# Rotary tables scaled once per layer, the norms' rounding and remainder on other engines, and ScalarE's squares ahead of its mask

## The reference

```python
# stacked: x = x + 0.5 * ffn_stack(layernorm(x)); x = x + ssm_block(layernorm(x)); x = x + 0.5 * ffn_stack(layernorm(x))
# x is (8, 256, 128); DIM = 128, DEPTH = 6, HEADS = 16, DIM_HEAD = 64, WINDOW = 32, QK_SCALE = 8.0
def attn_layer(x, Wqkv, qs, ksc, Wo):
    q, k, v = jnp.split(x @ Wqkv, 3, -1)          # heads of 64
    q = l2norm(q) * qs                            # norm over each head's 64 values, then a scale per layer and feature
    k = l2norm(k) * ksc
    q = q * cos * scale + rotate_half(q) * sin * scale
    k = k * cos * inv + rotate_half(k) * sin * inv          # inv = 1 / scale
    out = local_attention(q, k, v)                # windows of 32 queries, the window's and the previous window's keys
    return out @ Wo

def local_attention(q, k, v):
    sim = jnp.einsum('bhwie,bhwje->bhwij', bq, bk2) * QK_SCALE
    sim = jnp.where(mask, -jnp.finfo(sim.dtype).max, sim)
    attn = jax.nn.softmax(sim, -1)
    return jnp.einsum('bhwij,bhwje->bhwie', attn, bv2)

for i in range(DEPTH):
    x = attn_layer(shift_tokens(x), Wqkv[i], q_scale[i], k_scale[i], Wo[i]) + x
    x = ffn_layer(shift_tokens(x), ln_g[i], ln_b[i], W1[i], b1[i], W2[i], b2[i]) + x
```

## Time and profile before

| what | value |
|---|---|
| median of three runs | 3386.6 us |
| lowest, highest run | 3373.16, 3394.69 us |
| span of the profiled execution | 3373.6 us |
| TensorE (PE) busy | 2905.4 us, 86% |
| VectorE (DVE) busy | 2981.4 us, 88% |
| ScalarE (ACT) busy | 2061.4 us, 61% |
| GpSimd (POOL) busy | 2425.2 us, 72% |
| mean granted TensorE clock | 0.938 |

### The profile page before, as it was taken

How to read it: one execution, slowest core, us unless ns; L and a number is a source line. 1 busy time by engine, 2 the same in 40 slices (tenths; PEclk the granted TensorE clock), 3 DMA queues, 4 the chain that set the end, 5 groups by cost and what they waited for, 6 DMA issues and landing times. The chain is left out here.

```text
span 3373.6 us, 132100 instructions
## 1 busy us (share of the span) xinstructions
PE 2905.4 (86%) x57914; PEld 1846.3 (55%) x57914; DVE 2981.4 (88%) x4200; ACT 2061.4 (61%) x3820; POOL 2425.2 (72%) x1679
## 2 busy tenths in 40 slices
PE   5788889989989899987767788998999988999987
PEld 3455555655655555653323455565566655565653
DVE  6789899999999899896898878989999989899994
ACT  3466566666666665664764456666666666566663
POOL 3678777787787687774454667778788787787773
PEclk8899999999999999998887889999999999999998
DMA  5233332333333333320001333333343333333330
GB/s 140 65 83 73 82 91 68 89 90 72 86 92 71 84 85 71 83 72 28 7 7 44 80 72 79 75 87 86 75 97 76 90 84 72 81 94 71 86 76 14
DMA packets 114726, 250.85 MB, mean 74 GB/s; under 512 B 27244, under 2 KB 60648, under 8 KB 114152
## 3 DMA queue, kind: packets, MB, share of 16 engines
q1 hardware_dynamic: 114152, 242.40, 30.3%
HBM read 37.82 MB, written 3.15 MB: 12 GB/s over the span
## 5 line engine op out<-in xcount | busy, mean ns | idle before, releaser
L1085 ACT ACTIVATE squares<-general 128x512 f32<-128x512 f32 x768 | 453.9, 597 | 720.8 <-PE general L658 712.2
L1279 POOL TENSOR_TENSOR probs<-probs,row_sum 128x1024 f32<-128x1024 f32 x192 | 365.3, 1903 | 426.3 <-DVE row_sum L957 425.5
L1259 POOL TENSOR_TENSOR q_ring<-q_ring,partner 128x512 f32<-128x512 f32 x384 | 491.1, 1279 | 216.6 <-DMA partner<-sines 216.3
L868 DVE SCALAR_TENSOR_TENSOR sines<-general,vec,consts 128x512 f32<-128x512 f32 x768 | 560.7, 730 | 68.4 <-ACT squares L1085 65.5
L1259 POOL TENSOR_TENSOR k_ring<-k_ring,partner 128x512 f32<-128x512 f32 x384 | 490.8, 1278 | 0.0
L692 PE MATMUL general<-probs_t,v_buf 32*64 32x64 f32 x24576 | 339.4, 236 | 158.3 <-issue 87.0
L656 PE MATMUL general<-xs_hi,wqkv_lo 128*128 128x512 f32 x768 | 457.3, 595 | 15.8 <-DVE xs_lo L897 7.6
L692 PEld LDWEIGHTS general<-probs_t,v_buf 32*64 32x64 f32 x24576 | 305.6, 135 | 248.8 <-issue 241.7
L1273 POOL TENSOR_TENSOR probs<-probs,q_scale 128x1024 f32<-128x1024 f32 x192 | 365.3, 1903 | 15.1
L668 PE MATMUL general<-att,wo 128*128 128x512 f32 x768 | 370.4, 627 | 6.5 <-ACT att L1155 5.2
L719 PE MATMUL general<-k_ring,q_ring 64*32 64x64 f32 (+1 forms) x24576 | 294.2, 224 | 88.4 <-issue 53.5
(11 more groups left out here) (232 smaller groups left out, 6348.2 us busy)
## 6 DMA issues: line engine op xcount, KB each, us to landing
partner<-sines SPq DMA_DIRECT2D x1536, 128.0 KB, 2.3
wqkv_raw<-in_wqkv SPq DMA_DIRECT2D x80, 208.0 KB, 2.7
wo<-in_wo SPq DMA_DIRECT2D x12, 512.0 KB, 5.1
w<-in_w SPq DMA_DIRECT2D x12, 341.0 KB, 3.2
base_dram<-x SPq DMA_DIRECT2D x8, 256.0 KB, 2.4
att<-in_wqkv SPq DMA_DIRECT2D x2, 1024.0 KB, 6.1
sines<-base_dram SPq DMA_DIRECT2D x8, 256.0 KB, 4.0
w<-in_w SPq DMA_DIRECT2D x12, 128.0 KB
```

The costliest lines, as they stand in the source:

```text
L868: e.scalar_tensor_tensor(out=by_seq(sines[:, i % 2, which, :]), in0=g, scalar=scale, in1=both(tables[:, 2 * which + 1, :]), op0=ALU.mult, ...
L1085: e.activation(squares[:, (2 * p + which) % 4, :], general_of(("proj", k, n, p, which))[:, :], ACT.Square).then_inc(S[f"squared_{side}"], 1)
L1259: e.tensor_tensor(y, y, partner[:, i % 2, which, :], ALU.add).then_inc(S[f"rotated_{side}"], 1)
L1279: e.tensor_tensor(y, y, spread_keys(row_sum[:, i % 2, :]), ALU.mult).then_inc(S["probs_done"], 1)
```

## The change

It has three parts.

First, the product of rotary table and per-layer scale is made once per layer: `dve_tables` writes `layer_tables` (two tables of 256 columns each for queries, and two for keys, at the first item of a layer), and the four rotary instructions of a step become plain tensor_tensor products with it. `inv_norm` becomes a part of `k_inv`, and the state-space weights `mw` and `wbc` are loaded into `wqkv_raw`, after the last projection weights of the first stack have been split; their DMAs move on SP's queue from before the first stack's steps to behind them.

Second, ScalarE writes the rounded root itself (`high`, an activation with `F32R` output) and the root beside it, both ahead of the eight roots for the queries; GpSimd subtracts (`pool_norms_low`, behind `pool_scores`); VectorE only transposes, and that later in its step, behind `dve_turn`. `dve_var` and `dve_norms`, which overwrite `norm_t`, now also wait until the queries' scales of the item before have been read from it (`q_scaled`).

Third, in each step ScalarE squares the queries' projection first and writes the mask afterwards.

```diff
-xs_hi xs_lo proj_q proj_k squared_q squared_k cos_q cos_k sin_q sin_k moved0 moved1 rotated_q rotated_k
+xs_hi xs_lo tables_scaled proj_q proj_k squared_q squared_k cos_q cos_k sin_q sin_k moved0 moved1 rotated_q rotated_k
...
+        layer_tables = sb("layer_tables", [P, 4, SEQ])
...
-        inv_norm = sb("inv_norm", [P, COLS])
+        inv_norm = k_inv[:, WIN:]
...
-        mw = sb("mw", [P, 4, P])
-        wbc = sb("wbc", [P, P])
+        raw_words = wqkv_raw.rearrange("p i c -> p (i c)")
+        mw = raw_words[:, 0:4 * P].rearrange("p (m n) -> p m n", m=4)
+        wbc = raw_words[:, 4 * P:5 * P]
...
+            if k == 0:
+                w.wait_ge(S["wqkv_lo"], DEPTH * PAIRS)
+                e.dma_start(mw, mw_in.rearrange("m d n -> d m n")).then_inc(S["m_loaded"], 16)
+                e.dma_start(wbc, wb_in).then_inc(S["m_loaded"], 16)
+                e.dma_start(mvec[:, :], mvec_in).then_inc(S["m_loaded"], 16)
...
+        def dve_tables(e, w, k, layer, which):
+
+            w.wait_ge(S["vec_loaded"], 16)
+            w.wait_ge(S[f"cos_{SIDE[which]}"], (k * ITEMS + layer * CHUNKS) * PAIRS)
+            cut = slice(2 * which, 2 * which + 2)
+            e.tensor_scalar(layer_tables[:, cut, :], tables[:, cut, :], vcol(layer, V_QS + which), None, ALU.mult)\
+                .then_inc(S["tables_scaled"], 1)
+
         def dve_rotate(e, w, k, n, p, which):
...
-            g, scale = by_seq(general_of(("proj", k, n, p, which))[:, :]), vcol(layer, V_QS + which)
-            w.wait_ge(S["vec_loaded"], 16)
+            g = by_seq(general_of(("proj", k, n, p, which))[:, :])
+            if p == 0 and n % CHUNKS == 0:
+                dve_tables(e, w, k, layer, which)
+            w.wait_ge(S["tables_scaled"], 2 * (k * DEPTH + layer) + which + 1)
             w.wait_ge(S[f"squared_{side}"], i + 1)
...
-            e.scalar_tensor_tensor(out=by_seq(sines[:, i % 2, which, :]), in0=g, scalar=scale, in1=both(tables[:, 2 * which + 1, :]),
-                                   op0=ALU.mult, op1=ALU.mult).then_inc(S[f"sin_{side}"], 1)
+            e.tensor_tensor(by_seq(sines[:, i % 2, which, :]), g, both(layer_tables[:, 2 * which + 1, :]), ALU.mult).then_inc(S[f"sin_{side}"], 1)
...
-            e.scalar_tensor_tensor(out=by_seq(qk_ring[which][:, slot_of(n, p), :]), in0=g, scalar=scale,
-                                   in1=both(tables[:, 2 * which, :]), op0=ALU.mult, op1=ALU.mult).then_inc(S[f"cos_{side}"], 1)
+            e.tensor_tensor(by_seq(qk_ring[which][:, slot_of(n, p), :]), g, both(layer_tables[:, 2 * which, :]), ALU.mult).then_inc(S[f"cos_{side}"], 1)
...
+            w.wait_ge(S["q_scaled"], m * 8)
...
         def dve_norms_back(e, w, k, n):
 
             m = k * ITEMS + n
-            w.wait_ge(S["k_root"], m + 1)
-            root, low, high = (norm_t[:, :, i * NORM_ROWS:(i + 1) * NORM_ROWS] for i in range(3))
-            e.tensor_copy(high.bitcast(F32R), root).then_inc(S["norms_high"], 1)
-            w.wait_ge(S["norms_high"], m + 1)
-            e.tensor_tensor(low, root, high, ALU.subtract).then_inc(S["norms_low"], 1)
             w.wait_ge(S["norms_low"], m + 1)
-            w.wait_ge(S["inv_parts"], m)
-            e.transpose(inv_norm[:, :], norm_t.rearrange("p w h -> p (w h)")).then_inc(S["k_norms_turned"], 1)
+            w.wait_ge(S["k_norms_off"], 2 * m * GROUPS)
+            e.transpose(inv_norm, norm_t.rearrange("p w h -> p (w h)")).then_inc(S["k_norms_turned"], 1)
...
         def act_norms(e, w, k, n):
             m = k * ITEMS + n
             w.wait_ge(S["sums_inverted"], m + 1)
+            inverse, low, high, root = (norm_t[:, :, i * NORM_ROWS:(i + 1) * NORM_ROWS] for i in range(4))
+            e.activation(high.bitcast(F32R), inverse, ACT.Sqrt).then_inc(S["norms_high"], 1)
+            e.activation(root, inverse, ACT.Sqrt).then_inc(S["k_root"], 1)
...
-            w.wait_ge(S["q_scaled"], (m + 1) * 8)
-            e.activation(norm_t[:, :, 0:NORM_ROWS], norm_t[:, :, 0:NORM_ROWS], ACT.Sqrt).then_inc(S["k_root"], 1)
...
             for st in PLAN:
+                if st.now:
+                    act_square(e, w, k, *st.now, 0)
                 if st.scores:
                     act_mask(e, w, k, *st.scores)
-                if st.now:
-                    act_square(e, w, k, *st.now, 0)
...
+        def pool_norms_low(e, w, k, n):
+            m = k * ITEMS + n
+            low, high, root = (norm_t[:, :, i * NORM_ROWS:(i + 1) * NORM_ROWS] for i in range(1, 4))
+            w.wait_ge(S["norms_high"], m + 1)
+            w.wait_ge(S["k_root"], m + 1)
+            e.tensor_tensor(low, root, high, ALU.subtract).then_inc(S["norms_low"], 1)
...
                 if st.off:
                     pool_scores(e, w, k, *st.off)
+                if st.norms_back is not None:
+                    pool_norms_low(e, w, k, st.norms_back)
```

More of the change, by code:

```diff
@@ L541, in sync_stack @@
             load_w2(e, w, k, 0)
-            if k == 0:
-                e.dma_start(mw[:, :, :], mw_in.rearrange("m d n -> d m n")).then_inc(S["m_loaded"], 16)
-                e.dma_start(wbc[:, :], wb_in).then_inc(S["m_loaded"], 16)
-                e.dma_start(mvec[:, :], mvec_in).then_inc(S["m_loaded"], 16)
-            else:
+            if k:
                 store_bases(e, w, k)
@@ L843, in dve_var @@
             w.wait_ge(S["k_norms_turned"], turned["norms"])
+            w.wait_ge(S["q_scaled"], turned["norms"] * 8)
             e.transpose(var_t.rearrange("p w k -> p (w k)"), general_of(("var", key))[:, :]).then_inc(S["ln_var_kept"], 1)
@@ L1004, in vector_stack @@
                         dve_hidden(e, w, k, st.values_of[0], j)
-                if st.norms_back is not None:
-                    dve_norms_back(e, w, k, st.norms_back)
                 if st.first_split is not None:
@@ L1022, in vector_stack @@
                     dve_turn(e, w, k, *st.turn)
+                if st.norms_back is not None:
+                    dve_norms_back(e, w, k, st.norms_back)
                 if st.norms is not None:
@@ L1120, in act_norms_high @@
             w.wait_ge(S["norm_spread"], m * GROUPS)
-            e.activation(inv_parts[:, :], inv_norm[:, :], ACT.Copy).then_inc(S["inv_parts"], 1)
+            e.activation(inv_parts[:, :], inv_norm, ACT.Copy).then_inc(S["inv_parts"], 1)
         def act_gelus(e, w, k, n):
@@ L1387, in tensor_part @@
                     g = pe_bank(w, ("m_bc", c))
-                    e.matmul(g[:, :], wbc[:, :], m_u[c], start=True, stop=True).then_inc(S["m_bc"], 1)
+                    e.matmul(g[:, :], wbc, m_u[c], start=True, stop=True).then_inc(S["m_bc"], 1)
         def pe_added(e, w, at):
```

## The result

The changed kernel takes 3685.8 us in the median of four runs (3668.0 to 3689.3), the kernel before, measured beside it, 3380.0 us: a ratio of 1.089, 95% interval 1.085 to 1.094. The forecast was 3339 us, its range ended at 3480, and its largest rival on the slow side stood at 3497.

The account below looks back on a forecast made before the run. VectorE was taken as first bound (57.3 us an item), TensorE close second (56.0). With VectorE relieved, TensorE's 58.4 to 63.0 us gave a middle of 60.7, 48 us less over 48 items: 3339 us, range 3230 to 3480.

Parts of the forecast that it names:

- its largest rival on the slow side: TensorE's clock falls to half rate after the new gaps; one fall in two groups gives 3497 us; chance 0.30.
- VectorE's saving: Rotary products 82.8 us less, table products 11.2 more, norms 155.0 less: 226.6 us net, 4.72 us an item.
- The gap before the scores: TensorE's scores start later behind ScalarE's squares and mask: 1.25 us mean over four groups, 5.0 us an item.
- The sum: TensorE's need sets the time: 58.4 to 63.0 us an item, middle 60.7, 1.0 us less than before.
- The lower end: TensorE's 56.0 us busy less 2.6 of hidden waits plus 5.0 for the mask: 58.4 us an item, 3228 us.
- the upper end: TensorE's 56.0 us busy, 5.0 for the mask, 2.0 of issue before the values product: 63.0 an item, 3449 us.
- The norms' chain: GpSimd's subtraction and the later transpose make TensorE's spread 0 to 2.1 us late an item, 100 us in all; taken as 0.
- The rival in which part two does not hold: Norms' chain late by 1 to 2 us an item, 3387 to 3435 us, or rotary products no cheaper; chance 0.18.
- VectorE as no bound: After the change VectorE needs 52.6 us an item in place of 57.3 and no longer bounds; TensorE does.
- The case in which all of the saving arrives: TensorE's round trip for the mask falls into time it would have waited anyhow: 3160 us; chance 0.17.
- The clock's rival: TensorE's granted clock halves after new gaps, 1.65 us a fall; 96 falls cost 158 us, 3497 us; chance 0.30.
- The signs set down in advance: Products near 682 ns, VectorE busy some 200 us less and idler than TensorE, its transpose waits about 1 us at most, mask waits about 100.

Follow-up runs that it names:

- e2: The kernel before with part three alone (queries squared before the mask is written): 3582.1 us, ratio 1.062 to the kernel before.
- e7: e3 plus ScalarE's rounding ahead of the eight roots; VectorE still subtracts and transposes at the old place, mask first: 3325.0 us, ratio 0.986.
- e12: e7 with part three added (queries squared before the mask): 3556.4 us, ratio 1.059 to the kernel before.
- e1: The changed kernel with part three alone undone (mask written before the squares): 3480.5 us, ratio 1.031 to the kernel before.
- e3: The kernel before with part one alone (scaled tables, shared memory, moved loads): 3364.4 us, ratio 0.997.
- e8: The changed kernel with TensorE writing all masks, so no score waits for ScalarE's mask: 3452.7 us, ratio 1.023 to the kernel before.
- e4: The kernel before with part two alone, keeping part one's shared memory and moved loads, mask first: 3500.1 us, ratio 1.037.
- e5: e1 with GpSimd's subtraction moved ahead of pool_sub and VectorE's transpose ahead of dve_turn: 3385.2 us, ratio 1.007 to the kernel before.
- e9: The kernel before with VectorE computing the queries' sine product twice in even steps: 3463.0 us, ratio 1.032.
- e11: The kernel before with VectorE computing the keys' sine product twice in odd steps: 3472.1 us, ratio 1.033.
- e10: e7 with TensorE writing all masks itself: 3324.4 us, ratio 0.989 to the kernel before.

## Why the prediction was wrong

**VectorE's saving: right by instructions, a little less in busy time.** The groups of the changed kernel:

```profile
L882 DVE TENSOR_TENSOR sines<-general,layer_tables 128x512 f32<-128x512 f32 x768 | 517.5, 674 | 298.5 <-ACT squares L1093 295.7 <-DMA partner<-sines 1.6
L887 DVE TENSOR_TENSOR k_ring<-general,layer_tables 128x512 f32<-128x512 f32 x384 | 260.6, 679 | 0.0
L887 DVE TENSOR_TENSOR q_ring<-general,layer_tables 128x512 f32<-128x512 f32 x384 | 260.0, 677 | 0.0
L869 DVE TENSOR_SCALAR layer_tables<-consts,vec 128x512 f32<-128x512 f32 x24 | 17.2, 718 | 0.3 <-DVEq L838 0.3
```

The products take 1038.1 us, 92 less than before, where 82.8 had been worked out from L940; the table products take 17.2 us, between 11.2 and 34.1. With the norms' 132.3 us of cast and subtraction that makes 207 us less, where the prediction's terms make 204. The busy time fell by 170.2: neighbours overlap in the trace (a cosine product starts before the sine product has ended) and busy time counts an overlap once. All of VectorE's groups together fell by 200 us, the overlap by 30.

**The gap before the scores: right in place and size.** One group of the changed kernel (start, length; the wait in brackets):

```profile
1327.78 0.39 PE L661 MATMUL general<-xs_hi,wqkv_hi 128*128 128x512 f32 x1
...
1328.01 0.39 PE L741 MATMUL general<-inv_parts,spread_sel 128*128 128x256 f32 x2
...
1328.21 0.60 ACT L1093 ACTIVATE squares<-general 128x512 f32<-128x512 f32 x1 [1.59 <-PE general L661]
...
1328.70 1.11 ACT L1146 ACTIVATE general<-mask_bf 128x512 f32<-128x512 bf16 x2
...
1329.96 1.50 PE L722 MATMUL general<-k_ring,q_ring 64*32 64x32 f32 x128 [1.56 <-ACT general L1146]
```

The projection ends, the squares run, the masks follow from 1328.70 to 1329.81, and the scores start 0.15 us later after 1.56 us of waiting. I had 1.6 us for such a group, 1.25 in the mean of 192 and 240 us in all; the waits grew by 227.6 us here, by 241.5 us in `e2` and by 249.0 us from `e7` to `e12`.

**The sum: this step failed.** I let TensorE absorb the gap. The lower end took 2.6 us an item out of its busy time as hidden waits and dropped all issue waits; the upper end dropped the issue waits before the scores; and the forecast was the middle, 60.7 us. The item took 69.1. In the middle of the second stack (2200 to 3500 us, 18.8 items; the waits there are 108.5, 28.1, 22.4 and 37.0 us in the order of the table) it is made up so, rounded, beside the upper end's 63.0:

| us an item | upper end | measured |
|---|---|---|
| TensorE busy | 56.0 | 57.8 |
| scores waiting for the mask | 5.0 | 5.8 |
| issue before the values product | 2.0 | 1.5 |
| issue before the scores | 0 | 1.2 |
| spread waiting for `inv_parts` | 0 | 2.0 |
| other waits | 0 | 0.9 |

So 2.3 of the missing 8.4 us come from taking the middle: the time that I had counted as waits hidden in busy time did not shrink. The spread's 2.0 us had been entered as nothing, the issue waits before the scores are still there (1.2), and TensorE's busy time rose by 1.8. What the gap did absorb is the wait for `cos_q`, 1.0 us an item, which both ends had dropped:

| part three added | mask waits | waits for `cos_q` | time |
|---|---|---|---|
| to the kernel before (`e2`) | +241.5 | -45.2 | +207 |
| to the rest of the change (`e1`) | +217.6 | -44.6 | +200 |
| to `e7` (`e12`) | +249.0 | -50.7 | +229 |

It does not go because VectorE is relieved: it is 52.5 us in `e3`, 54.5 in `e1`, 61.7 in `e7` and 57.0 in `e8`, all with less work for VectorE, and 9.1 in `e2`, where VectorE has all of it. It goes wherever TensorE stands before the scores, which fits a VectorE that catches up meanwhile. The right sum was the time before, plus the added waits at their full length, minus the waits for VectorE that come later in the same step.

**The norms' chain: priced right and entered as nothing.** I had worked out 2.1 us late for the spread, 100 us in all, and took 0 since a relieved VectorE would start the chain earlier. The waits grew by 88.0 us, in `e4` alone by 99.4. The rival in which part two does not hold had 48 to 96 us for this, so it had the right cause and size, but it stood as a case of its own and not in the sum. A step of the changed kernel shows why nothing came earlier:

```profile
1042.09 1.83 ACT L1136 ACTIVATE hidden<-general,vec 128x512 f32<-128x512 f32 x3
...
1042.73 0.39 PE L661 MATMUL general<-xs_hi,wqkv_hi 128*128 128x512 f32 x1
...
1043.67 1.90 POOL L1289 TENSOR_TENSOR probs<-probs,q_scale 128x1024 f32<-128x1024 f32 x1
...
1043.82 0.59 ACT L1093 ACTIVATE squares<-general 128x512 f32<-128x512 f32 x1
...
1044.44 0.69 DVE L882 TENSOR_TENSOR sines<-general,layer_tables 128x512 f32<-128x512 f32 x1 [3.06 <-ACT squares L1093]
...
1045.53 0.46 POOL L1275 TENSOR_TENSOR norm_t<-norm_t 128x128 f32<-128x128 f32 x1
...
1045.65 1.23 DVE L974 STREAM_TRANSPOSE probs_t<-probs 128x1024 f32<-128x1024 f32 x1
...
1046.81 0.67 DVE L935 STREAM_TRANSPOSE k_inv<-norm_t 128x512 f32<-128x512 f32 x1
...
1047.51 0.63 ACT L1130 ACTIVATE inv_parts<-k_inv 128x512 fp32r<-128x512 f32 x1 [3.10 <-DVE k_inv L935]
...
1048.29 0.47 PE L741 MATMUL general<-inv_parts,spread_sel 128*128 128x256 f32 x2 [1.88 <-ACT inv_parts L1130]
```

GpSimd's subtraction comes at the place I had given it, behind the product that ends at 1045.57 (0.46 us, in the range of 0.32 to 1.28). But before that VectorE had stood 3.06 us before the keys' rotary pair, waiting for ScalarE's squares of the keys: TensorE ended the keys' projection only at 1043.12, and ScalarE was then still in a GELU until 1043.92. VectorE's transposition of the probabilities comes next, from 1045.65, and the norms' transpose only at 1046.81, another 0.8 us after GpSimd was done. The transpose was put behind two things that wait for others. `e5` moves both places and gets 85 us back.

**VectorE as no bound: only half right.** `e3` brought 10 us for some 90 us of products, so the saving does not arrive while TensorE is as full. But `e9` and `e11` show that VectorE bounds too. The case in which all of the saving arrives was given 0.17 on the ground that VectorE is the busier engine; that ground holds for what is added, not for what is taken away.

**The clock: a small part.** The granted clock is 0.923 in the mean in place of 0.938. A clock of 0.923 means half rate for 0.154 of 3681 us, 567 us, one of 0.938 for 0.124 of 3374, 418 us; the 149 us more cost at most 74 us of work, and TensorE's busy time grew by 58.7. The rival had needed one fall in two groups, 158 us. In `e2`, with all of the mask's gaps, the clock is 0.938: the gaps alone do not bring it down. The Trainium skill ("TensorE: Matmul & The Clock Gate", "A second HAM failure mode: psum-queue depth-cycling") says that frequent short idles between groups of matmuls make the clock swing; the 241.5 us of such idles added in `e2` did not make it swing more, so here the rule does not decide. The clock's rival, 3497 us, came nearest of all that had been written down, but for a reason that is worth at most 74 of the 307 us; that it had the sign right is luck. Why the clock is lower in some kernels stays open: `e1` and `e4`, with some 108 and 110 us of waits for `inv_parts`, have 0.926 and 0.924, but `e8` has 0.941 with 107 us of them, and the doses `e9` and `e11` have 0.929 and 0.930 with hardly any.

The signs set down in advance read: VectorE's products at about 682 ns (674 to 679) and its busy time down by some 200 us (170.2); scores' waits for the mask up to about 100 us in 1200, which is 5.1 us an item (262.3 us over 48 items, 5.5 each); VectorE with more idle time than TensorE (870 us against 717); no wait of VectorE before the norms' transpose over about 1 us. The last was not quite met: 13.9 us in 7 waits, up to 4.4 us, none before the other 41. It was the wrong thing to watch, since part two's cost stood on TensorE's side.

## What to carry to other kernels

When two engines are both over 90% busy and run in lockstep, price an addition to either at its full length and a saving on one of them at little. Of a new wait take off only the waits for the other engine that come later in the same step, and let no part of it vanish into idle time whose cause isn't known. Before the order of a helper engine is changed, look who waits for the later of the two things: here a mask that needed nothing from the step was put behind a result of the same step, and this turned a write done ahead into a round trip of 1.6 us on the fullest engine. Work taken from a full engine should stay where its input is early and nothing queued before it waits for others: the same rounding on ScalarE gained 1.4% together with the tables (`e7`) and lost 3.7% by itself where the remainder went to GpSimd and the transpose behind two waits (`e4`).

## What the runs showed of the hardware that had not been expected

- VectorE's subtraction over 128 columns, both inputs in SBUF, lasts until the GpSimd instruction beside it has ended, and 0.15 us more: 48 of 48 in the kernel before (1862 ns in the mean, mostly beside products of 1.90 us) and 48 of 48 in `e7` (1154 ns, mostly beside rotary additions of 1.28 us). GpSimd does the same subtraction in 0.46 us.
- TensorE's bf16 masks of 512 columns cost about their pitch between float32 matmuls: 366 more of them made it busy 69.5 us longer in `e10`, 0.19 us each.
- The waits that part three adds before the scores, 241.5 us in `e2`, left the mean granted clock at 0.938.
